# Attention inside a macaron block: TensorE's order of scores, exponents and values in rounds of two units

## The chip, the cores and the metric

The kernel runs on one core of one Trainium2 chip. The metric is the device time of one execution in microseconds (us), median of three runs. A profiled execution gives the trace; its span (first to last instruction) is a little shorter than the device time.

## What is computed

A macaron block on x of shape 8 x 512 x 128: half an attention-and-mixture-of-experts layer, a recurrence, the same half layer again. Cut to the part that the change touches, run twice in the kernel:

```python
def _msa(x, w_qkv, w_proj):              # H = 16 heads of DK = 8, on layer-normed x
    qkv = (x @ w_qkv).reshape(b, n, 3, H, DK)
    q, k, v = ...                        # each b, h, n, d; n = 512
    attn = jnp.einsum('bhnd,bhmd->bhnm', q, k) * (1.0 / np.sqrt(DK))
    attn = jax.nn.softmax(attn, axis=-1)
    y = jnp.einsum('bhnm,bhmd->bhnd', attn, v)
    return y.transpose(0, 2, 1, 3).reshape(b, n, d) @ w_proj
...
x = x + 0.5 * _L0_ffn_ref(_layernorm(x), ...)   # holds _msa and the experts
x = x + _L0_attn_ref(_layernorm(x), ...)        # recurrence, no change here
x = x + 0.5 * _L0_ffn_ref(_layernorm(x), ...)
```

## The kernel before

`attention_phase` (line 461) is written by hand for five engines; each has its own instruction stream, and semaphores join them. Work is cut into batches (8), groups of four heads (4 to a batch, so 32 groups in all, counted by G) and units: unit u of a group is 128 of the 512 keys for the four heads. A step handles one group: its four units' exponents and values, and, two groups ahead, the scores from which the softmax maxima come.

In each unit TensorE (`step`, line 727) issues four pairs and one set of values. Pair n is a score matmul (`score`, line 657: 62 rows, 512 columns, for group G + 2) and an exponent matmul (`exponent`, line 685: 64 rows, 512 columns, for group G). The two use different halves of the array's rows and run beside each other. The values (`pv`, line 691) are four matmuls of 128 rows by 32 columns, one per head, side by side; each stands in the trace as two instructions. In before they come in two halves of 256 columns, `part` 0 and 1. The order in a unit is: pairs 0 and 1, half the values of the unit before, pairs 2 and 3, the other half; in unit 1 the first half comes behind pair 2.

The scores go to four PSUM banks (`psS`, line 500): score h to bank h. VectorE reduces two banks at a time to maxima over 512 (`reduce_pair`, line 830; line 834): first scores 0 and 1, then 2 and 3. Score 0 and score 2 wait for VectorE: lines 659 and 660 let a score into its bank only when the reduction of the same two banks, of the unit before, has ended; `s_read` counts reductions.

The exponents go through a ring of three banks (`RING`, lines 509 to 516), which they share with the turned maxima ("m") and the turned outputs ("o"). ScalarE reads each one and writes probabilities (line 816). The outputs of two groups (`SHARE`) accumulate in bank 7; after them ScalarE copies the bank (`keep_o`, line 787), TensorE turns the copy (`turn_o`, line 709, four transposes), ScalarE copies the result (`copy_o`, line 793), and GpSimd divides by the sums (`normalize`, line 618: a power at line 621 and two products at line 627).

The maxima of a group go through GpSimd (`split_max`, line 608), TensorE (`turn_max`, line 705), ScalarE (`keep_rows`, line 781) and two DMAs of SP (`place`, line 559) into two extra rows of the queries, so that the exponent matmul subtracts them. The exponents of a group wait for that (line 733). In before `turn_max` is at the end of unit 0, `turn_o` at the end of unit 1 of an even group.

Before the first step a prelude computes the scores of groups 0 and 1 alone (lines 715 to 724), with `turn_max(1)` between the two. In the last two groups no scores are left.

Of the kernel before, what the change touches and what calls it, by code (L numbers as in the profile page):

```python
# [13 lines left out]
P = 128  # L14
# [446 lines left out]
def attention_phase(nc, ps, s, v_all, y_all, qd, kd, load=None):  # L461
# [4 lines left out]
    with Phase(nc) as ctx:  # L466
# [13 lines left out]
        neg_wide = sb("neg_wide", [P, P], F32R)  # L480
        neg_parts = neg_wide[:, 0:NMAX].rearrange("p (e a m) -> p e a m", e=2, a=SPLITS)
# [28 lines left out]
        for u in range(TPB):  # L510
            RING += [("e", u, 0), ("e", u, 1)]
            RING += [("e", u, 2), ("e", u, 3)]
            if u == 0:
                RING.append(("m",))
            if u == 1:
                RING.append(("o",))
# [25 lines left out]
        with nc.Block() as block:  # L542
# [46 lines left out]
            def _(pool):  # L589
# [10 lines left out]
                g_.memset(neg_wide[:, NMAX:].bitcast(F32), 0.0).then_inc(v_set, 1)  # L600
# [31 lines left out]
                pool.wait_ge(v_set, NG + 2)  # L632
# [5 lines left out]
                def step(b, g, first, last):  # L638
                    if not first or g > 0:
# [5 lines left out]
                        if g % SHARE == 0:  # L645
                            normalize(bb, gg - 1, shared(b, g))
# [7 lines left out]
            def _(pe):  # L654
# [36 lines left out]
                def pv(g, u, unit, part):  # L691

                    if part == 0:
                        pe.wait_ge(e_read, 4 * unit + 4)
                    here = slice(part * T // 2, (part + 1) * T // 2)


                    for h in range(GROUP):
                        last = t.matmul(psO[VW * h:VW * (h + 1), here], vs[g][:, u, h, :], probs[u % 2][:, h, here],  # L699
                                        start=(g % SHARE == 0 and u == 0 and part == 0),  # L700
                                        stop=(g % SHARE == SHARE - 1 and u == TPB - 1 and part == 1))
                    if part:
                        last.then_inc(pv_unit, 1)

                def turn_max(count):
                    pe.wait_ge(split_done, count)
                    t.transpose(ring("m")[:, 0:P], neg_wide[:].bitcast(F32), s["ident"][:]).then_inc(rows_turned, 1)
# [7 lines left out]
                for i in range(2):  # L715
# [6 lines left out]
                    if i == 0:  # L722
                        pe.wait_ge(v_set, NG + 2)
                        turn_max(1)
                pe.wait_ge(q_set, 3 * NG)

                def step(b, g, first, last):
# [3 lines left out]
                    for u in range(TPB):  # L731
# [10 lines left out]
                        def values(part):  # L742
                            if u > 0:
                                if u == 1 and part == 0:
                                    pe.wait_ge(v_staged, G + 1)
                                    if g % SHARE == 0 and not (first and g == 0):
                                        pe.wait_ge(o_kept, shared(b, g))
                                pv(g, u - 1, unit - 1, part)
                            elif not (first and g == 0):
                                pv((g - 1) % NG, TPB - 1, unit - 1, part)  # L750

                        ahead_score(0)
                        exponent(b, g, first, last, u, 0)
                        ahead_score(1)
                        exponent(b, g, first, last, u, 1)
                        if u != 1:
                            values(0)
                        ahead_score(2)
                        exponent(b, g, first, last, u, 2)
                        if u == 1:  # L760
                            values(0)
                        ahead_score(3)
                        exponent(b, g, first, last, u, 3)
                        values(1)
                        if u == 0 and not (last and g == NG - 1):
                            ring_free(b, g, first, last, "m")
                            turn_max(G + 2)
                        if u == 1 and g % SHARE == 0 and not (first and g == 0):
# [4 lines left out]
                for part in range(2):  # L773
                    pv(NG - 1, TPB - 1, TPB * NG * B - 1, part)
# [1318 lines left out]
```

## Time and profile before

| | |
|---|---|
| device time, median of 3 (range) | 1531.38 us (1530.72 to 1533.6) |
| the profiled execution: span | 1515.8 us |
| TensorE matmul, busy share of the span | 82% |
| VectorE | 70% |
| ScalarE | 56% |
| GpSimd | 43% |
| attention, first to last reduction, first time | 59.9 to 405.2 us |
| attention, first to last reduction, second time | 953.9 to 1299.4 us |

The profiled execution's own time is its span and 15.6 us around it, if it is taken to be the median. Busy time counts an instruction from its recorded start to its recorded end; instructions of an engine can overlap in it, and a group's mean length is then more than the spacing of starts. In rows of a timeline, the first number is the start in us from the start of the span, the second the length of the row's stretch, and "x4" the number of instructions merged in it; "[0.32 <-PE ps L661]" is the engine's idle time before the row and what ended it. PE is TensorE's matmuls, PEld its weight loads, DVE VectorE, ACT ScalarE, POOL GpSimd.

### The profile page before, as it was taken

What the parts mean: (1) busy time and instruction counts of PE and PEld (TensorE: products, weight loads), DVE (VectorE), ACT (ScalarE), POOL (GpSimd) and SP (SyncE); (2) the same over time, 40 slices, a digit from 0 to 9 for tenths busy, and PEclk for the clock granted to TensorE, in tenths of its full rate; (3) what the DMA queues carried; (4) which work ended last, traced back from release to release, by engine and by line L of the source; (5) the groups of instructions that cost most, each with busy time, mean ns of one, the idle gap of its engine ahead of it and who ended that gap; (6) DMA issues with size and microseconds to landing.
All of it is one profiled execution on the core that took longest, in us unless ns stands there. A gap on an engine that the chain in (4) does not pass through costs nothing. (4 is left out here: it accounts for less than half of the span.)

```text
span 1515.8 us, 39418 instructions
## 1 busy us (share of the span) xinstructions
PE 1245.9 (82%) x12592; PEld 708.5 (47%) x12593; DVE 1065.5 (70%) x1896; ACT 851.6 (56%) x1710; POOL 646.5 (43%) x743
## 2 busy tenths in 40 slices
PE   5499999999969497398888746699999999875793
PEld 3234343434349497144454434233443434375793
DVE  8689989998645232468888757799899989264232
ACT  3178888888831253444334214288888888720451
POOL 4312343233336465355765632323432343337362
PEclk9689999999985699599999859599999999965897
DMA  5513342212001121100000005221212111001124
GB/s 177 164 30 78 100 108 60 63 47 55 16 1 34 56 69 45 49 2 3 3 3 2 3 1 224 55 58 46 56 44 57 43 56 44 2 8 61 49 68 122
DMA packets 81640, 81.93 MB, mean 54 GB/s; under 512 B 16265, under 2 KB 53868, under 8 KB 81536
## 3 DMA queue, kind: packets, MB, share of 16 engines
q1 hardware_dynamic: 72704, 70.01, 16.7%
q0 software_dynamic: 4608, 8.44, 1.7%
q10 hardware_dynamic: 4224, 2.10, 0.5%
q8 instruction: 64, 1.05, 0.3%
q14 instruction: 40, 0.33, 0.1%
HBM read 50.56 MB, written 29.93 MB: 53 GB/s over the span
## 5 line engine op out<-in xcount | busy, mean ns | idle before, releaser
L834 DVE TENSOR_REDUCE maxima<-ps 128x2 f32<-128x1024 f32 x512 | 623.9, 1225 | 73.9 <-PE ps L661 68.3
L816 ACT ACTIVATE probs<-ps 128x512 f32<-128x512 f32 x1024 | 552.8, 594 | 92.5 <-PE ps L688 76.2
L661 PE MATMUL ps<-k_stack,q_stack 62*128 62x512 f32 x1024 | 384.4, 474 | 35.2 <-DMA k_stack<-k_split 24.0
L688 PE MATMUL ps<-q_stack,k_stack 64*128 64x512 f32 x1024 | 385.0, 458 | 0.4
L699 PE MATMUL ps<-probs,v_stack 128*32 128x256 f32 x4096 | 329.3, 394 | 1.2 <-ACT probs L816 1.2
L661 PEld LDWEIGHTS ps<-k_stack,q_stack 62*128 62x128 f32 x1024 | 158.6, 194 | 232.8 <-DVE maxima L834 118.2
L621 POOL TENSOR_TENSOR inv<-o_rows,minus_one 128x32 f32<-128x32 f32 x32 | 174.1, 5439 | 132.4 <-ACT o_rows L797 132.4
L688 PEld LDWEIGHTS ps<-q_stack,k_stack 64*128 64x128 f32 x1024 | 160.3, 186 | 15.7 <-ACT probs L816 7.5
L699 PEld LDWEIGHTS ps<-probs,v_stack 128*32 128x32 f32 x4096 | 81.0, 108 | 169.7 <-issue 115.5
L613 POOL CAST neg_wide<-maxima 128x16 fp32r<-128x16 f32 x64 | 12.6, 196 | 302.1 <-DVE maxima L834 302.1
L1314 POOL DMA_INDIRECT expert_out<-yt,number x80 | 78.4, 979 | 69.4 <-POOL number L1310 35.0
L1291 DVE COPY w_now<-w 128x512 f32 x80 | 34.2, 427 | 85.9 <-issue 43.5
L1272 ACT ACTIVATE xT<-ps,ln_b,ln_w 128x128 f32<-128x128 f32 x80 | 36.6, 457 | 95.3 <-PE ps L1243 95.3
L1249 PE MATMUL ps<-xT,w_now 128*128 128x128 f32 x640 | 88.6, 283 | 0.0
L1256 PE MATMUL ps<-w,hidT 128*128 x640 | 85.6, 278 | 0.0
L1249 PEld LDWEIGHTS ps<-xT,w_now 128*128 128x128 f32 x640 | 81.1, 199 | 0.0
L1256 PEld LDWEIGHTS ps<-w,hidT 128*128 128x128 f32 x640 | 79.2, 195 | 0.1
L1172 POOL DMA_INDIRECT sorted<-rows,slot x64 | 62.3, 973 | 18.3 <-issue 15.9
L1277 ACT ACTIVATE hidT<-ps 128x512 f32<-128x512 f32 x80 | 47.8, 598 | 37.0 <-PE ps L1249 37.0
L1746 POOL TENSOR_TENSOR r_kx<-r_kx,r_k_factor 128x512 f32<-128x512 f32 x48 | 61.0, 1271 | 11.4 <-PE ps L1924 7.7
L1727 POOL TENSOR_TENSOR r_mixed<-r_shift,zT 128x512 f32<-128x512 f32 x40 | 59.2, 1487 | 14.2 <-DVE r_shift L1603 14.2
L1243 PE MATMUL ps<-ident,xt 128*128 128x128 f32 x80 | 23.3, 291 | 44.1 <-DMA xt<-sorted 44.1
(204 smaller groups left out, 1673.7 us busy)
## 6 DMA issues: line engine op xcount, KB each, us to landing
q_stack<-q_split SPq DMA_DIRECT2D x256, 64.0 KB
k_stack<-k_split SPq DMA_DIRECT2D x512, 32.0 KB
q_split<-q_parts SPq DMA_DIRECT2D x16, 512.0 KB, 2.7
k_split<-k_parts SPq DMA_DIRECT2D x16, 512.0 KB, 3.4
xt<-sorted SPq DMA_DIRECT2D x80, 64.5 KB
w<-in_L_ffn_w SPq DMA_DIRECT2D x16, 256.0 KB, 3.1
rows<-expert_out SPq DMA_DIRECT2D x16, 256.0 KB, 3.3
x_all<-in_L_attn_x SPq DMA_DIRECT2D x8, 256.0 KB, 3.0
```

What stands on the lines that cost most here:

```text
L621: g_.tensor_tensor(inv[:].rearrange("p q h w -> p (q h w)"), o_rows[:].rearrange("p q h w d -> p (q h w) d")[:, :, DK], minus_one[:].rearr ...
L661: mm = t.matmul(psS[:, h, :], qs[g][score_rows(h), h // 2, u * P:(u + 1) * P], ks[g][score_rows(h), h // 2, :], start=True, stop=True)
L688: t.matmul(ring("e", u, n), ks[g][half(h), h // 2, u * P:(u + 1) * P], qs[g][half(h), h // 2, :], start=True, stop=True).then_inc(e_ready, 1)
L699: last = t.matmul(psO[VW * h:VW * (h + 1), here], vs[g][:, u, h, :], probs[u % 2][:, h, here], start=(g % SHARE == 0 and u == 0 and part = ...
L816: a.activation(probs[u % 2][:, h, :], ring("e", u, n), ACT.Exp, scale=float(DK) ** -0.5).then_inc(e_read, 1)
L834: v.tensor_reduce(maxima[i][:, :, pair, u:u + 1], psS[:, 2 * pair:2 * pair + 2, :], AX_X, ALU.max, negate=True).then_inc(s_read, 1)
L1172: pool.indirect_dma_start(xs, bass.IndirectOffsetOnAxis(ap=slot[:, i:i + 1], axis=0), rows[:, i, :], None).then_inc(scattered, 16)
L1249: last = t.matmul(psH[o][:, c * P:(c + 1) * P], w1_now[o][:, c * P:(c + 1) * P], xT[o][:], start=True, stop=True)
L1256: last = t.matmul(psY[i][:, 0:P], hidT[i][:, c, :], s["w2"][:, ds(second_expert, 1), c, :], start=(c == 0), stop=(c == HC - 1))
L1314: pool.indirect_dma_start(ys, bass.IndirectOffsetOnAxis(ap=number[out_slot][:], axis=0), yt[out_slot][:], None, bounds_check=TOK - 1, oob_ ...
L1727: g.tensor_tensor(mixed[f][:], shift[f % 2][:], x, ALU.add).then_inc(mixed_ready.sem, 1)
L1746: g.tensor_tensor(dst[:].rearrange("p (k m) -> p k m", m=m), src[:].rearrange("p (k m) -> p k m", m=m), k_factor[l][:].rearrange("p n two ...
```

## The change

Five things in `attention_phase`:

- TensorE's order. Two units make a round. Even unit: pairs 0, 1, 2, then all values of the unit before in one block of 512 columns, then pair 3. Odd unit: pairs 0 and 1, half the values, pairs 2 and 3, the other half. In unit 1 of an even group all values come behind pair 3, then the outputs are turned.
- `turn_max` moves from the end of unit 0 to the middle of unit 1, ahead of the values, and turns 32 columns instead of 128 (`neg_wide` shrinks); in the prelude it moves into the scores of group 1. The ring's order follows.
- ScalarE copies the outputs ahead of the last exponential of unit 0, not at the start of unit 1, and the turned maxima ahead of the third exponential of unit 1.
- GpSimd normalizes in the odd group that follows, not in the even group in which the outputs are turned.
- One memset on GpSimd goes, with the count that it stood for.

The diff, cut to its core:

```diff
-        neg_wide = sb("neg_wide", [P, P], F32R)
-        neg_parts = neg_wide[:, 0:NMAX].rearrange("p (e a m) -> p e a m", e=2, a=SPLITS)
+        neg_wide = sb("neg_wide", [P, NMAX], F32R)
+        neg_parts = neg_wide[:].rearrange("p (e a m) -> p e a m", e=2, a=SPLITS)
...
             RING += [("e", u, 0), ("e", u, 1)]
+            if u == 1:
+                RING.append(("m",))
             RING += [("e", u, 2), ("e", u, 3)]
-            if u == 0:
-                RING.append(("m",))
...
-                        if g % SHARE == 0:
-                            normalize(bb, gg - 1, shared(b, g))
+                    if g % SHARE and not (first and g == 1):
+                        bb, gg = (b, g - 2) if g > 1 else (b - 1, NG - 1)
+                        normalize(bb, gg - 1, shared(b, g))
...
-                def pv(g, u, unit, part):
-
-                    if part == 0:
+                def pv(g, u, unit, first, count):
+
+                    if first == 0:
                         pe.wait_ge(e_read, 4 * unit + 4)
-                    here = slice(part * T // 2, (part + 1) * T // 2)
+                    here = slice(first * T // 2, (first + count) * T // 2)
...
-                    t.transpose(ring("m")[:, 0:P], neg_wide[:].bitcast(F32), s["ident"][:]).then_inc(rows_turned, 1)
+                    t.transpose(ring("m")[0:NMAX, 0:P], neg_wide[:].bitcast(F32), s["ident"][:]).then_inc(rows_turned, 1)
...
-                    if i == 0:
-                        pe.wait_ge(v_set, NG + 2)
-                        turn_max(1)
+                        if i == 1 and u == 1:
+                            pe.wait_ge(v_set, NG + 1)
+                            turn_max(1)
...
-                        ahead_score(0)
-                        exponent(b, g, first, last, u, 0)
-                        ahead_score(1)
-                        exponent(b, g, first, last, u, 1)
-                        if u != 1:
-                            values(0)
-                        ahead_score(2)
-                        exponent(b, g, first, last, u, 2)
+                        def pair(n):
+                            ahead_score(n)
+                            exponent(b, g, first, last, u, n)
+
+                        pair(0)
+                        pair(1)
+                        if u % 2 == 0:
+                            pair(2)
+                            if u:
+                                pv(g, u - 1, unit - 1, 0, 2)
                             elif not (first and g == 0):
-                                pv((g - 1) % NG, TPB - 1, unit - 1, part)
...
+                                pv((g - 1) % NG, TPB - 1, unit - 1, 0, 2)
+                            pair(3)
+                            continue
                         if u == 1:
-                            values(0)
-                        ahead_score(3)
-                        exponent(b, g, first, last, u, 3)
-                        values(1)
-                        if u == 0 and not (last and g == NG - 1):
-                            ring_free(b, g, first, last, "m")
-                            turn_max(G + 2)
-                        if u == 1 and g % SHARE == 0 and not (first and g == 0):
+                            pe.wait_ge(v_staged, G + 1)
+                            if not (last and g == NG - 1):
+                                ring_free(b, g, first, last, "m")
+                                turn_max(G + 2)
+                        fresh = u == 1 and g % SHARE == 0
+                        if not fresh:
+                            pv(g, u - 1, unit - 1, 0, 1)
+                        pair(2)
+                        pair(3)
+                        if fresh:
+                            if not (first and g == 0):
+                                pe.wait_ge(o_kept, shared(b, g))
+                            pv(g, u - 1, unit - 1, 0, 2)
+                        else:
+                            pv(g, u - 1, unit - 1, 1, 1)
+                        if fresh and not (first and g == 0):
                             ring_free(b, g, first, last, "o")
                             turn_o(shared(b, g))
...
-                        if u == 1 and g % SHARE == 0 and not (first and g == 0):
-                            keep_o(shared(b, g))
-                        if u == 1 and not (last and g == NG - 1):
-                            keep_rows((g + 1) % 2, G + 2)
...
                         for n, h in enumerate(E_ORDER):
+                            if u == 0 and n == 3 and g % SHARE == 0 and not (first and g == 0):
+                                keep_o(shared(b, g))
+                            if u == 1 and n == 2 and not (last and g == NG - 1):
+                                keep_rows((g + 1) % 2, G + 2)
```

## Rows read from the trace of the kernel before

**Rows 1.** The page's costliest groups: count | busy, mean ns | idle before, releaser.
```profile
L834 DVE TENSOR_REDUCE maxima<-ps 128x2 f32<-128x1024 f32 x512 | 623.9, 1225 | 73.9 <-PE ps L661 68.3
L816 ACT ACTIVATE probs<-ps 128x512 f32<-128x512 f32 x1024 | 552.8, 594 | 92.5 <-PE ps L688 76.2
L661 PE MATMUL ps<-k_stack,q_stack 62*128 62x512 f32 x1024 | 384.4, 474 | 35.2 <-DMA k_stack<-k_split 24.0
...
L699 PE MATMUL ps<-probs,v_stack 128*32 128x256 f32 x4096 | 329.3, 394 | 1.2 <-ACT probs L816 1.2
L621 POOL TENSOR_TENSOR inv<-o_rows,minus_one 128x32 f32<-128x32 f32 x32 | 174.1, 5439 | 132.4 <-ACT o_rows L797 132.4
```
**Rows 2.** Windows: attention, its prelude, and a stretch of the recurrence (last row).
```profile
core 0: us, PE busy (x) PEld busy (x) DVE busy (x) ACT busy (x) POOL busy (x), PEclk, DMA share, GB/s
200.00:250.00 50.00, 49.10 (x459) 20.12 (x461) 45.34 (x38) 42.66 (x84) 17.75 (x24) 1.00 0.38 92
...
61.50:79.00 17.50, 10.78 (x29) 3.85 (x27) 15.38 (x14) 0.27 (x1) 5.54 (x15) 0.50 0.33 63
800.00:840.00 40.00, 32.59 (x780) 18.53 (x779) 35.81 (x65) 14.85 (x47) 26.65 (x20) 1.00 0.01 2
```
**Rows 3.** Timeline of VectorE, prelude and first group.
```profile
67.79 1.21 DVE L834 TENSOR_REDUCE maxima<-ps 128x2 f32<-128x1024 f32 x1
71.12 9.14 DVE L834 TENSOR_REDUCE maxima<-ps 128x2 f32<-128x1024 f32 x8 [2.12 <-PE ps L661]
...
85.52 1.23 DVE L834 TENSOR_REDUCE maxima<-ps 128x2 f32<-128x1024 f32 x1 [1.15 <-PE ps L661]
87.68 1.23 DVE L834 TENSOR_REDUCE maxima<-ps 128x2 f32<-128x1024 f32 x1 [0.94 <-PE ps L661]
```
**Rows 4.** Timeline of TensorE's weight loads, even group, units 0 to 2.
```profile
211.60 0.18 PEld L661 LDWEIGHTS ps<-k_stack,q_stack 62*128 62x128 f32 x1 [0.41 <-issue]
...
212.27 0.16 PEld L699 LDWEIGHTS ps<-probs,v_stack 128*32 128x32 f32 x8 [0.37 <-issue]
212.84 0.14 PEld L707 LDWEIGHTS ps<-ident,neg_wide 128*128 128x128 f32 x1 [0.41 <-ACT probs L816]
213.10 0.18 PEld L661 LDWEIGHTS ps<-k_stack,q_stack 62*128 62x128 f32 x1
...
213.66 0.18 PEld L661 LDWEIGHTS ps<-k_stack,q_stack 62*128 62x128 f32 x1 [0.19 <-DVE maxima L834]
...
214.32 0.16 PEld L699 LDWEIGHTS ps<-probs,v_stack 128*32 128x32 f32 x8 [0.24 <-ACT probs L816]
214.89 0.18 PEld L661 LDWEIGHTS ps<-k_stack,q_stack 62*128 62x128 f32 x1 [0.41 <-issue]
...
215.32 0.16 PEld L699 LDWEIGHTS ps<-probs,v_stack 128*32 128x32 f32 x8 [0.24 <-issue]
215.89 0.42 PEld L712 LDWEIGHTS ps<-ident,oT 128*128 128x128 f32 x4 [0.41 <-issue]
216.47 0.18 PEld L661 LDWEIGHTS ps<-k_stack,q_stack 62*128 62x128 f32 x1 [0.17 <-issue]
```
**Rows 5.** The same view, outputs turned six groups earlier.
```profile
151.12 0.42 PEld L712 LDWEIGHTS ps<-ident,oT 128*128 128x128 f32 x4 [0.41 <-issue]
```
**Rows 6.** Timeline of VectorE, the stretch of rows 4.
```profile
211.23 2.38 DVE L834 TENSOR_REDUCE maxima<-ps 128x2 f32<-128x1024 f32 x2
213.88 1.23 DVE L834 TENSOR_REDUCE maxima<-ps 128x2 f32<-128x1024 f32 x1 [0.27 <-PE ps L661]
215.43 1.23 DVE L834 TENSOR_REDUCE maxima<-ps 128x2 f32<-128x1024 f32 x1 [0.32 <-PE ps L661]
```
**Rows 7.** Timeline of TensorE's matmuls: the last two halves of values, with no work between.
```profile
424.57 1.07 PE L699 MATMUL ps<-probs,v_stack 128*32 128x256 f32 x16 [0.60 <-ACT probs L816]
```
**Rows 8.** Timelines of an odd group: turning of maxima, and VectorE behind it.
```profile
224.28 0.14 PEld L707 LDWEIGHTS ps<-ident,neg_wide 128*128 128x128 f32 x1 [0.77 <-ACT probs L816]
...
225.31 2.49 DVE L834 TENSOR_REDUCE maxima<-ps 128x2 f32<-128x1024 f32 x2 [0.63 <-PE ps L661]
```

More of the change, by code:

```diff
@@ L599, in _ @@
                     g_.memset(vs[i][:], 0.0).then_inc(v_set, 1)
-                g_.memset(neg_wide[:, NMAX:].bitcast(F32), 0.0).then_inc(v_set, 1)
                 g_.memset(minus_one[:], -1.0).then_inc(v_set, 1)
@@ L630, in normalize @@
                     last.then_inc(o_done, 1)
-                pool.wait_ge(v_set, NG + 2)
+                pool.wait_ge(v_set, NG + 1)
                 for g in range(NG):
@@ L689, in exponent @@
                              start=True, stop=True).then_inc(e_ready, 1)
-                def pv(g, u, unit, part):
-                    if part == 0:
+                def pv(g, u, unit, first, count):
+                    if first == 0:
                         pe.wait_ge(e_read, 4 * unit + 4)
-                    here = slice(part * T // 2, (part + 1) * T // 2)
+                    here = slice(first * T // 2, (first + count) * T // 2)
                     for h in range(GROUP):
                         last = t.matmul(psO[VW * h:VW * (h + 1), here], vs[g][:, u, h, :], probs[u % 2][:, h, here],
-                                        start=(g % SHARE == 0 and u == 0 and part == 0),
-                                        stop=(g % SHARE == SHARE - 1 and u == TPB - 1 and part == 1))
-                    if part:
+                                        start=(g % SHARE == 0 and u == 0 and first == 0),
+                                        stop=(g % SHARE == SHARE - 1 and u == TPB - 1))
+                    if first + count == 2:
                         last.then_inc(pv_unit, 1)
@@ L740, in ahead_score @@
                                 score(g2, u, h, 8 * (G + 2) + 2 * u + h // 2)
[L742 to L748, printed above, removed]
-                            elif not (first and g == 0):
-                                pv((g - 1) % NG, TPB - 1, unit - 1, part)
@@ L772, in _ @@
                 bodies(pe, step)
-                for part in range(2):
-                    pv(NG - 1, TPB - 1, TPB * NG * B - 1, part)
+                pv(NG - 1, TPB - 1, TPB * NG * B - 1, 0, 2)
                 turn_o(NG * B // SHARE)
```

## The prediction

> **What bounds the kernel now.** I read the costliest groups first. The reductions to maxima (VectorE), the exponentials (ScalarE) and the matmuls of scores and values, all of the attention phase, head the list [rows 1]. The windows then put numbers on one steady stretch: in 50 us TensorE is busy 49.10, VectorE 45.34, ScalarE 42.66, at the full granted clock [rows 2]. Two engines look like the bound, so the next question is how close VectorE really is. In the prelude, where reductions queue up behind each other, eight of them take 9.14 us and a single one 1.21, so the starts stand (9.14 - 1.21) / 7 = 1.13 apart, although each lasts 1.23 [rows 3]: the last tenth of one lies under the next. VectorE could thus take one every 1.13 us. In the steady stretch they come every 1.24, because TensorE delivers them so: from the first weight load of a run of two pairs to that of the values 0.67 (211.60 to 212.27), from there to the next work 0.57 (212.27 to 212.84), together 1.24 for half a unit [rows 4]. TensorE's order sets the pace now; VectorE has 0.11 to spare on each reduction.
>
> The period of two groups (eight units): the outputs are turned at 151.12 and again at 215.89, six groups later [rows 5, 4]; 64.77 / 3 = 21.59 us. Of that, 16 half units are 19.84; the rest is the turning of maxima (0.26 each, 212.84 to 213.10), that of outputs (0.58, 215.89 to 216.47) and waits.
>
> One of these waits matters most. In the even group's second unit the program before already has a run of three: score 2 is issued there before the first values. At 213.66 its weight load waits for VectorE [rows 4]: the reduction that still reads banks 2 and 3 ends at 211.23 + 2.38 = 213.61 [rows 6]. Score 3 of that unit comes behind the values at 214.89, and the reduction of both starts at 215.43, after an idle 0.32 [rows 4, 6].
>
> **What the change does to TensorE alone.** A run of n pairs costs 0.43 for one (214.89 to 215.32) and 0.67 for two, so 0.24 for each more and 0.91 for three [rows 4]. The values of one unit in a single block are never seen in before. Four sets of four matmuls back to back take 1.07 with 0.38 for the last one's own length [rows 7], a set each 0.23; four sets and the change of shape behind them (0.57 less two sets, 0.11) make 1.03. A wide set saves a start or two, so I take 0.99; bounds are 0.92 (without the 0.11) and 1.14 (two halves of 0.57). A round of two units was 4 x 1.24 = 4.96 and becomes 0.91 + 0.99 + 0.91 + 0.57 + 0.67 + 0.57 = 4.62: one change of shape less, 0.34 saved.
>
> The Trainium skill, "TensorEngine Tiling (Array Packing)", Key Properties, says that changing the tiling mode drains the TensorE. By that rule the round ought to be 0.34 shorter, and the kernel faster (first rival).
>
> **What it does to the hand-over with VectorE.** The scores have four banks: 0 and 1 for scores 0 and 1, 2 and 3 for scores 2 and 3. One reduction reads two banks and needs both scores; score 2 of a unit may not start before the reduction of banks 2 and 3 of the unit before has ended. Before, scores 2 and 3 stand next to each other in three of four units. After, in every even unit (0 and 2), the whole block of values stands between them. So a chain forms that no slack elsewhere shortens, from the end of one reduction of banks 2 and 3 to the start of the next:
> - reduction's end to the weight load of score 2: 213.61 to 213.66, 0.05 [rows 6, 4];
> - that load to the load of the values: a run that starts anew behind a wait costs what a single pair does, 0.43;
> - the block of values: 0.99;
> - the load of score 3 to the reduction: 214.89 to 215.43, 0.54 [rows 4, 6].
> Sum 2.01. During it VectorE has only the reduction of banks 0 and 1, 1.13: it idles some 0.9 in each even unit. The round is then 2.01 plus the three reductions behind it: 1.13 + 1.13 until the next may start, 1.23 for the last, which has to end: 3.49. Round: 5.50, against 4.96 before. With the block at 0.92 it is 5.43; were the spacing 1.23, as busy times suggest, 5.70; with both upper ends 5.85. I take the queued spacing of 1.13, because reductions do queue there.
>
> TensorE needs only 4.62 of the 5.50 and waits for the rest. In the odd unit, score 2 waits until 1.23 + 0.05 = 1.28 after the even unit's second reduction starts; score 3 follows and both are ready well before VectorE has done the next reduction (0.67 - 0.43 + 0.54 = 0.78 later, at 2.06, against 2.26). That part adds nothing.
>
> **The round that turns outputs** (second unit of an even group): counted from the start of the first unit's second reduction, score 2 at 1.28, run of two 0.67, block 0.99, turning of outputs 0.58, run of three 0.91, block 0.99, score 3 to reduction 0.54: 5.96. TensorE is the bound in it.
>
> **The other parts.** Turning the maxima (0.26 or less, 32 columns of weights for 128) moves from a round's open path to a place ahead of score 2, which waits anyway until 1.28: nothing, as long as that wait is there, else 0.26 a group. The copy of turned maxima and that of outputs on ScalarE move by less than a unit; behind them stand exponentials. Eight of these cost at most 8 x 0.594 = 4.75 a round [rows 1], under 5.50: nothing. SP's placing of the maxima waits for that copy and comes about a unit later, ahead of the next loads in SP's queue; its result is wanted at the next group's start: nothing, and if it came late, TensorE would start that group later by as much. The normalization on GpSimd (5.44 for the power [rows 1]) goes to the odd group, where the copies of outputs are long done; behind it on GpSimd stands the splitting of maxima, which waits for the group's last reduction in any case. This removes the odd group's late turning (load at 224.28 behind 0.77 idle, VectorE idle 0.63) [rows 8], a gap that the period of 21.59 contains. The smaller zeroing on GpSimd is at the start, off the path.
>
> The prelude: VectorE's idle 2.12 between the two groups [rows 3] goes, since the turning comes inside the second group's scores: -2.1 per attention. Against it stands the start at the lower clock, where reductions are 2.16 apart (85.52 to 87.68) [rows 3]: a block and a turn of twice the length on the same chain, about +2 (0 to 3) in the first two groups, which also lack one block and one turning of outputs. Both together: nothing.
>
> **Sum.** Two groups: 3 x 5.50 + 5.96 = 22.46, against 21.59: +0.87. Of 32 groups 30 have scores ahead; without the first two that is 14 such periods per attention, 28 in all: 28 x 0.87 = 24.4. The last two groups without scores run at ScalarE's and TensorE's exchange; I leave them. The profiled execution (1515.8 span and 15.6 around it) stands for the median of 1531.38: 1531.4 + 24 = 1555.
>
> **Rivals.**
> 1. Faster: TensorE's own time decides, as now. Then the periods go to two rounds of 4.62, one with a turn of maxima 4.88, and one with both turns and two blocks 0.91 + 0.99 + 0.91 + 0.26 + 0.67 + 0.99 + 0.58 = 5.31: 19.43, or -2.16 x 28 = -60, and -4 in the preludes: 1467. It decides if the four links fit under the 1.13 of one reduction; the block alone takes 0.99. The wait at 213.66 and the idle 0.32 behind a half block speak against it. 0.06. The drain rule above leads here.
> 2. A shorter chain: each round 0.2 less than worked out, by links that overlap, gives 28 x (0.87 - 0.80) = 2 and thus 1533; nothing shows such an overlap. 0.08, half of it below 1528.
> 3. The spacing is 1.23, or the block 1.14: round 5.70 or 5.65, 1572 or 1568. Against the first of the two stands a steady row, two reductions in 2.38 and so 2.38 - 1.23 = 1.15 apart [rows 6]. 0.10.
> 4. TensorE waits more, and its clock falls to 1.2 GHz for part of the phase. It would be busy 4.62 of 5.50, 84%; another stretch at 81% (32.59 of 40) keeps the full clock, while the prelude, with 10.78 of 17.50, is at half [rows 2]. A tenth of the rounds at half would add at least 12 x 4 = 48: 1600. 0.03. The Trainium skill, "TensorE: Matmul & The Clock Gate", section "A second HAM failure mode: psum-queue depth-cycling", describes a kernel whose short idles between groups of matmuls made the clock swing.
>
> **How the numbers follow.** The forecast, 1545 to 1565, has 0.73. The range reaches down to 1540 (block 0.92 and part of the turn hidden) and up to 1575 (third rival). What a measurement can tell from no change is about 0.2%, 3 us. Faster: 0.06 and 0.04, 0.10. Same: 0.04. Slower: the rest, 0.86.
>
> **What would show it.** In the profile after: in every even unit VectorE idles about 0.9 before the reduction of banks 2 and 3 and nothing before the next two; the weight load of score 2 is put down to the reduction; the block of values lasts near 0.99; periods of two groups near 22.5. If periods are below 21.6 with VectorE gap-free, rival 1 holds and my chain is wrong; if the gap is there but the reductions are 1.23 apart, rival 3.

## The result and the profile after

The changed kernel is slower: 1575.1 us, median of four runs (1568.4 to 1580.0), against 1531.05 for the kernel before (four runs, 1529.4 to 1533.6). The ratio is 1.0297, with a 95% interval of 1.0271 to 1.0323. The profiled execution after has a span of 1575.4 and a device time of 1577.2. The forecast was 1555, in a range of 1545 to 1565: the direction is right, but of +44 us it saw +24, and the result lies above the range.

The page's costliest groups first (columns as in [rows 1]):
```profile
L837 DVE TENSOR_REDUCE maxima<-ps 128x2 f32<-128x1024 f32 x512 | 597.2, 1221 | 135.7 <-PE ps L661 135.7
L819 ACT ACTIVATE probs<-ps 128x512 f32<-128x512 f32 x1024 | 543.7, 599 | 122.9 <-PE ps L688 118.1
L661 PE MATMUL ps<-k_stack,q_stack 62*128 62x512 f32 x1024 | 378.5, 468 | 55.3 <-DVE maxima L837 30.8
...
L620 POOL TENSOR_TENSOR inv<-o_rows,minus_one 128x32 f32<-128x32 f32 x32 | 174.1, 5442 | 34.9 <-ACT o_rows L800 34.9
```
All durations are within 2% of [rows 1]; the idle times are not. VectorE idles 135.7 before its reductions where it idled 73.9, all of it put down to the scores, and TensorE's scores wait more for VectorE (30.8 us, in before 11.1). Each of the two waits for the other, more than before. That VectorE's busy time falls from 623.9 to 597.2 at the same length of one reduction (1225 and 1221 ns) is no saving: reductions that queue lie over each other by a tenth (four in 4.69 below start (4.69 - 1.23) / 3 = 1.15 apart and last 1.23), and time in which two lie over each other counts once. GpSimd's wait for the copied outputs is down from 132.4 to 34.9, as the later normalization wants it.

The window of [rows 2] in the steady stretch, columns as there:
```profile
200.00:250.00 50.00, 46.28 (x350) 18.37 (x351) 40.85 (x35) 39.63 (x79) 15.33 (x18) 1.00 0.34 80
```
TensorE falls from 49.10 to 46.28 of 50 and VectorE from 45.34 to 40.85, at the full granted clock: no engine is busy throughout any more.

VectorE's timeline shows the rounds (start, length, then how many reductions queue without a gap, and the idle time ahead of them):
```profile
201.82 4.62 DVE L837 TENSOR_REDUCE maxima<-ps 128x2 f32<-128x1024 f32 x4 [0.53 <-PE ps L661]
207.40 4.69 DVE L837 TENSOR_REDUCE maxima<-ps 128x2 f32<-128x1024 f32 x4 [0.96 <-PE ps L661]
212.91 4.68 DVE L837 TENSOR_REDUCE maxima<-ps 128x2 f32<-128x1024 f32 x4 [0.82 <-PE ps L661]
218.49 3.49 DVE L837 TENSOR_REDUCE maxima<-ps 128x2 f32<-128x1024 f32 x3 [0.90 <-PE ps L661]
223.07 1.23 DVE L837 TENSOR_REDUCE maxima<-ps 128x2 f32<-128x1024 f32 x1 [1.09 <-PE ps L661]
224.83 1.23 DVE L837 TENSOR_REDUCE maxima<-ps 128x2 f32<-128x1024 f32 x1 [0.53 <-PE ps L661]
```
Each row but that at 223.07 begins with the second reduction of an even unit, so the distance of two is a round: 207.40 - 201.82 = 5.58, then 5.51, then 5.58, and the round that turns outputs 224.83 - 218.49 = 6.34. The idle 0.8 to 1.0 stands before the second reduction of an even unit, and nothing before those behind it, as forecast, except behind the turning of outputs (1.09 at 223.07, 0.53 at 201.82 and 224.83). The row at 218.49 has exactly the three reductions of the forecast, and they take the forecast 3.49.

How the 44 us divide, from the starts and ends of these instructions in the two profiled executions (us, each of the two attentions within 0.1):

| stretch of one attention | before | after | difference | forecast |
|---|---|---|---|---|
| first reduction to first exponential (prelude) | 20.25 | 18.04 | -2.2 | -2.1 |
| first exponential to that of the third group | 22.91 | 23.16 | +0.25 | +2 |
| 14 periods of two groups, each | 21.58 | 22.96 | +1.38 | +0.87 |
| last reduction to last exponential (tail) | 19.27 | 21.63 | +2.4 | 0 |
| last exponential to last output | 9.43 | 9.43 | 0 | 0 |

For both attentions the ends of these stretches are 39.4 apart from those before (19.7 each). The other +5 of the medians' +44 lies outside attention, by this account.

### The profile page after: what moved, and what is told of

The parts are those of the page before. It is cut to its first block and busy times, and to the rows that moved or that the text cites. A ratio compares the mean times of both kernels' runs of the same rounds, so it can differ in the third digit from the quotient of the medians.

```text
span 1575.4 us, 36848 instructions
## 1 busy us (share of the span) xinstructions
PE 1254.6 (80%) x11312; PEld 707.7 (45%) x11313; DVE 1042.7 (66%) x1896; ACT 842.1 (53%) x1710; POOL 646.3 (41%) x741
## 5 line engine op out<-in xcount | busy, mean ns | idle before, releaser
L837 DVE TENSOR_REDUCE maxima<-ps 128x2 f32<-128x1024 f32 x512 | 597.2, 1221 | 135.7 <-PE ps L661 135.7
L819 ACT ACTIVATE probs<-ps 128x512 f32<-128x512 f32 x1024 | 543.7, 599 | 122.9 <-PE ps L688 118.1
L661 PE MATMUL ps<-k_stack,q_stack 62*128 62x512 f32 x1024 | 378.5, 468 | 55.3 <-DVE maxima L837 30.8
L688 PE MATMUL ps<-q_stack,k_stack 64*128 64x512 f32 x1024 | 374.1, 459 | 0.3 <-ACT probs L819 0.3
L699 PE MATMUL ps<-probs,v_stack 128*32 128x512 f32 (+1 forms) x2816 | 296.2, 493 | 18.4 <-ACT probs L819 18.4
L661 PEld LDWEIGHTS ps<-k_stack,q_stack 62*128 62x128 f32 x1024 | 168.6, 194 | 297.6 <-DVE maxima L837 155.5
L620 POOL TENSOR_TENSOR inv<-o_rows,minus_one 128x32 f32<-128x32 f32 x32 | 174.1, 5442 | 34.9 <-ACT o_rows L800 34.9
L688 PEld LDWEIGHTS ps<-q_stack,k_stack 64*128 64x128 f32 x1024 | 168.0, 187 | 25.7 <-ACT probs L819 14.0
L699 PEld LDWEIGHTS ps<-probs,v_stack 128*32 128x32 f32 x2816 | 55.5, 108 | 122.8 <-ACT probs L819 66.8
L1299 DVE COPY yt<-ps 128x128 f32<-128x128 f32 x80 | 23.3, 292 | 51.8 <-PE ps L1259 51.1
```

The source lines that it names most:

```text
L620: g_.tensor_tensor(inv[:].rearrange("p q h w -> p (q h w)"), o_rows[:].rearrange("p q h w d -> p (q h w) d")[:, :, DK], minus_one[:].rearr ...
L661: mm = t.matmul(psS[:, h, :], qs[g][score_rows(h), h // 2, u * P:(u + 1) * P], ks[g][score_rows(h), h // 2, :], start=True, stop=True)
L688: t.matmul(ring("e", u, n), ks[g][half(h), h // 2, u * P:(u + 1) * P], qs[g][half(h), h // 2, :], start=True, stop=True).then_inc(e_ready, 1)
L819: a.activation(probs[u % 2][:, h, :], ring("e", u, n), ACT.Exp, scale=float(DK) ** -0.5).then_inc(e_read, 1)
L837: v.tensor_reduce(maxima[i][:, :, pair, u:u + 1], psS[:, 2 * pair:2 * pair + 2, :], AX_X, ALU.max, negate=True).then_inc(s_read, 1)
```

## The experiments

All kernels are edits of the kernel before or after; ratios are to runs of the kernel before on the same chip. "Period" is two groups, "round" is two units, both averaged over an attention (median or mean moves them by a few hundredths). e4 and e6 to e9 are single executions: their device times have no interval, and they are read by periods.

**e1: break the chain at score 3.** In even units of after, score 3 goes ahead of the block of values; its exponent stays behind.
```diff
                             pair(2)
+                            ahead_score(3)
                             if u:
                                 pv(g, u - 1, unit - 1, 0, 2)
...
-                            pair(3)
+                            exponent(b, g, first, last, u, 3)
...
```


> The changed kernel with one move: in even units score 3 is issued ahead of the block of values, its exponent stays behind it. As many changes of shape, as many matmuls, ScalarE and GpSimd untouched. Theory (the block between scores 2 and 3 makes VectorE wait): the idle 0.96 us before the second reduction of even units goes, the chain is about 0.9 instead of 2.09, TensorE sets the pace again at 4.62 + 0.24 (score 3 without a partner) a round; two groups take about 20.8 instead of 22.96, device time about 1515 us. Rival (wider block, ScalarE's moved copies or the turn in mid-round make it slow): the period stays within 0.3 of 22.96 or rises by the lone score, 4 x 0.24 = 1 us, device time 1575 to 1600.

Measured: 1582.4, ratio 1.0355 (1.0326 to 1.0385), period 23.31. The expectation failed, though the idle 0.96 on VectorE fell to 0.2. Three rounds are at 5.21, 5.77 and 5.47, together 0.2 less than in after; the turning round is at 6.82 for 6.30. The weight loads, with the matching rows of VectorE and ScalarE behind them, show why:
```profile
202.73 0.19 PEld L688 LDWEIGHTS ps<-q_stack,k_stack 64*128 64x128 f32 x2 [0.84 <-ACT probs L820]
...
203.92 0.16 PEld L699 LDWEIGHTS ps<-probs,v_stack 128*32 128x32 f32 x8 [0.66 <-ACT probs L820]
204.49 0.18 PEld L661 LDWEIGHTS ps<-k_stack,q_stack 62*128 62x128 f32 x1 [0.41 <-issue]
...
206.55 0.18 PEld L661 LDWEIGHTS ps<-k_stack,q_stack 62*128 62x128 f32 x1 [0.52 <-DVE maxima L838]
...
208.28 0.19 PEld L688 LDWEIGHTS ps<-q_stack,k_stack 64*128 64x128 f32 x2 [0.84 <-ACT probs L820]
...
205.27 3.59 DVE L838 TENSOR_REDUCE maxima<-ps 128x2 f32<-128x1024 f32 x3 [0.49 <-PE ps L661]
...
203.27 1.58 ACT L820 ACTIVATE probs<-ps 128x512 f32<-128x512 f32 x3 [0.65 <-PE ps L688]
```
Exponent 3 is loaded behind the block (202.73), ScalarE begins on it at 203.27, and the next values may not start before it is through (203.92). Only behind those come the odd unit's scores 2 and 3 (204.49), their reduction (205.27), the next score 2 (206.55), and a block again (from 207.28 to 208.28): 208.28 - 202.73 = 5.55. There is a second loop, through ScalarE and VectorE, nearly as long as the first. What I had put in the list of parts as "nothing" (exponentials "under 5.50") is no chain by its sum of 4.75, but it is one by the place of exponent 3.

**e2: halves in even units again.** Pairs 0 to 2, half the values, pair 3, the other half.
```diff
                             if u:
-                                pv(g, u - 1, unit - 1, 0, 2)
+                                pv(g, u - 1, unit - 1, 0, 1)
...
                             pair(3)
+                            if u:
+                                pv(g, u - 1, unit - 1, 1, 1)
...
```


> The changed kernel with the block of even units cut in two: half behind pair 2, half behind pair 3, so four changes of shape a round as in the kernel before. Theory: the chain loses half a block, 0.43, so each round that the chain sets becomes 0.43 shorter (5.58 to 5.15), the round that turns outputs less; two groups about 21.6 us, device time about 1540. Rival (what counts is TensorE's changes of shape): one more change in each round, 4 x 0.34 longer, two groups 24.3, device time about 1612.

Measured: 1571.5, ratio 1.0283 (1.0246 to 1.0319), period 23.09: neither number. The chain from one reduction's end to the next one's start did become shorter, 1.66 in place of 2.09, but the rounds only 5.36 (odd group, into the second even unit 5.50), and the turning round grew from 6.30 to 6.84, which eats what the others gain. Between an odd unit's score 3 and the next even unit's score 2 stand a half and two pairs of TensorE's work, 1.48; the reduction needs 0.44 (until it starts) + 1.23 + 0.05 = 1.72 there. As the third pair of its run, score 2 comes too early whatever stands behind it, and TensorE waits in order.

**e5: score 3 and exponent 3 both ahead of the block**, the edit that shortens both loops.
```diff
                             pair(2)
+                            pair(3)
                             if u:
                                 pv(g, u - 1, unit - 1, 0, 2)
...
-                            pair(3)
```


> The changed kernel with all of pair 3 (score and exponent) ahead of the block of values in even units; still three changes of shape a round. Enlarged theory: TensorE issues in order, and two waits go round with the block: score 2, third in a run, waits for a reduction that started only 0.44 after the last score 3, and the next values wait for ScalarE to read exponent 3, which stands behind the block. This edit takes away the second and the block between scores 2 and 3, and leaves a wait of score 2 of about 0.3 a round: round 4.63 + 0.3 to 0.4, about 5.0; two groups 21.4 to 21.8 us, device time 1525 to 1540. Rival (the wide block itself, or fewer changes of shape, cost more than their rows say): two groups stay at 22.9 or more.

Measured: 1562.6, ratio 1.0229 (1.0190 to 1.0269), period 22.55 where 21.4 to 21.8 was expected. Three rounds are at 5.10, 5.12 and 5.38, near the 5.0 expected: with both loops cut the 5.5 goes. The round that turns outputs missed: 6.96. There `keep_o` stands in ScalarE's queue ahead of exponential 3, which is now ready before the block ends, and the copy needs the block:
```profile
215.53 0.60 ACT L794 ACTIVATE oT<-ps 128x512 f32<-128x512 f32 x1 [0.70 <-PE ps L699]
```

**e6 and e7: reductions over half the columns**, in after and in before. The maxima are those of the first 256 of 512 keys; the rest of the kernel is whole.
```diff
-  psS[:, 2 * pair:2 * pair + 2, :], AX_X,
+  psS[:, 2 * pair:2 * pair + 2, 0:T // 2], AX_X,
```


> The changed kernel with reductions over 256 of the 512 columns: the maxima are those of half the keys, all else is as it was. A reduction then lasts about 0.69 instead of 1.23. Theory (score 2 waits for VectorE): that wait goes, what is left is the values' wait for ScalarE; rounds of 5.58 become about 4.9, the round that turns outputs stays at 6.3; two groups 21.1 instead of 22.96. Rival (VectorE is not in the loop): two groups within 0.2 of 22.96.

> The kernel before with the same half reductions (maxima of half the keys). Theory: TensorE alone sets the pace there, so the period of two groups stays within 0.3 of 21.58, lower only by the waits of score 2 in the second unit of even groups. Rival (VectorE, busy 0.9, is a second bound): the period falls by 1 us or more.

Measured: in before the period stays at 21.58 (1516.4 us, a shorter prelude and less elsewhere): VectorE was no bound there, as read from [rows 4, 6]. In after the period falls from 22.96 to 21.49 and the rounds into a unit 0 from 5.58 to 4.91, the odd group's other one from 5.50 to 5.35 (1524.8 us); the turning round stays at 6.32. (21.1 was expected; the odd group's other round makes the difference.) So the lost time runs through the reductions, except in the turning round. The group of reductions in e6, and one load of values:
```profile
L837 DVE TENSOR_REDUCE maxima<-ps 128x2 f32<-128x512 f32 x512 | 342.0, 690 | 337.7 <-PE ps L661 337.7
...
200.18 0.16 PEld L699 LDWEIGHTS ps<-probs,v_stack 128*32 128x32 f32 x8 [0.68 <-ACT probs L819]
```
VectorE is out of the way, and the rounds are still 4.91, not TensorE's 4.62: the values wait for ScalarE.

**e8: the outputs' copy twice on ScalarE** (after, with a spare tile).
```diff
+                    a.activation(oT_more[:], psO, ACT.Copy)
                     a.activation(oT[:], psO, ACT.Copy).then_inc(o_kept, 1)
```


> The changed kernel with ScalarE's copy of the outputs made twice (the first into a spare tile). It stands ahead of exponential 3 of the first unit of even groups. Theory (this copy delays exponentials 3, 0 and 1, by these the bank for exponent 3 and so the second block): the round that turns outputs grows by the 0.48 of one more copy, 6.30 to 6.78, the others stay at 5.50 to 5.58. Rival (ScalarE has slack, as the prediction had it): nothing changes.

Measured: the turning round goes from 6.30 to 6.79, the others stay at 5.50 to 5.58, the period is 23.45 (1593.3 us). ScalarE in one such round:
```profile
196.86 0.60 ACT L795 ACTIVATE oT_more<-ps 128x512 f32<-128x512 f32 x1 [0.40 <-PE ps L700]
197.35 0.59 ACT L796 ACTIVATE oT<-ps 128x512 f32<-128x512 f32 x1
197.83 1.58 ACT L821 ACTIVATE probs<-ps 128x512 f32<-128x512 f32 x3
```
The second copy begins 0.49 after the first and puts the exponentials back by 0.48; the round grows by 0.49, the whole of it. ScalarE's copy lies on the path of this round.

**e3 and e11: the change without its order** (the same kernel twice, e11 in more runs): before, with the normalization a group later and the turn of maxima inside the prelude's second group, and nothing else.
```diff
-                        if g % SHARE == 0:
-                            normalize(bb, gg - 1, shared(b, g))
+                    if g % SHARE and not (first and g == 1):
+                        bb, gg = (b, g - 2) if g > 1 else (b - 1, NG - 1)
+                        normalize(bb, gg - 1, shared(b, g))
...
-                    if i == 0:
...
+                        if i == 1 and u == 1:
...
+                            turn_max(1)
```


> The kernel before with two parts of the change alone: normalization on GpSimd in the odd group, and the turning of maxima in the prelude inside the second group's scores. TensorE's order in the steps is that of before. Theory: the late turning of maxima in odd groups goes, VectorE's idle 0.62 there falls to about 0.26 (the turn itself), two groups 21.59 to about 21.2; the first exponential of each attention comes 2.2 us earlier; device time 1531 - 30 x 0.18 - 4.4, about 1521. Rival (GpSimd's lateness was hidden by other waits): period unchanged, 1527 from the prelude alone.

> Kernel e3 again, in more rounds and on the same chip as e10: about 1516 us, 0.9901 of the kernel before, interval inside 0.985 to 0.995; two groups 21.31 us.

Measured: 1516.5, ratio 0.9901 (0.9866 to 0.9936), and 1514.9, ratio 0.9914 (0.9895 to 0.9934): faster than both kernels, and about 1% under the kernel before. The period is 21.31 in both, the prelude 18.04 as in after. 28 x (21.58 - 21.31) = 7.6 and 2 x 2.2 make 12 of the 13 to 15 us. GpSimd in an odd group of e3, and VectorE behind the turning of maxima, in this group (223.79) and in the even one that follows (234.03):
```profile
223.32 5.45 POOL L621 TENSOR_TENSOR inv<-o_rows,minus_one 128x32 f32<-128x32 f32 x1
...
231.48 0.20 POOL L613 CAST neg_wide<-maxima 128x16 fp32r<-128x16 f32 x1 [1.60 <-DVE maxima L835]
...
223.79 9.97 DVE L835 TENSOR_REDUCE maxima<-ps 128x2 f32<-128x1024 f32 x8 [0.27 <-PE ps L662]
234.03 1.23 DVE L835 TENSOR_REDUCE maxima<-ps 128x2 f32<-128x1024 f32 x1 [0.27 <-PE ps L662]
```
The power is over well before the group's last reduction, the splitting waits for VectorE alone (1.60 idle), and VectorE's 0.63 of [rows 8] is down to 0.27. Both parts are in after too, so what its order costs has to be measured against e3: 22.96 - 21.31 = 1.65 a period, or 46 us in 28.

**e10: e3, with the odd group's unit 1 in the even order of halves** (`values(0)` behind pair 1 there too).

> Kernel e3 (before with the normalization in odd groups and the turn inside the prelude) with one more edit: in unit 1 of odd groups the first half of the values goes behind pair 1, as in units 0, 2 and 3, so that no run of three is left there. Theory (a run of three makes score 2 wait): VectorE's idle 0.09 before the second reduction of that unit goes; two groups 21.31 to about 21.2 us, 3 us in the device time. Rival (what counts is the number of changes of shape, equal in both): no difference.

Measured: 1526.1, ratio 0.9977 (0.9960 to 0.9994), period 21.45, slower than e3's 21.31 on the same chip. The idle 0.09 that it aimed at goes to 0.01, but 0.235 appears before the second reduction of unit 2: the gap moves on and grows. The 28 x 0.14 = 4 us of the periods and 1 us in the two tails are less than half of the 11 us between e10 and e11; the rest was not traced.

**e9: halves in the last two groups of after**, which have no scores.
```diff
+                        if not ahead:
+                            prior = (g, u - 1) if u else ((g - 1) % NG, TPB - 1)
+                            pair(0)
+                            pair(1)
...
+                            else:
+                                pv(*prior, unit - 1, 0, 1)
+                            pair(2)
...
+                            pair(3)
+                            pv(*prior, unit - 1, 1, 1)
...
```
(In unit 1 the first half comes behind pair 2, and the turns and the copies stand where after has them.)

> The changed kernel, but in the last two groups, which have no scores ahead, the values go in halves as in the kernel before (behind pair 1, or behind pair 2 in unit 1, and behind pair 3). Theory (the block and the later turn leave ScalarE idle in this tail): the time from the last reduction to the last exponential falls from 21.6 to about 19.3 us, all else stays. Rival (a spell at the lower clock after the last reduction is to blame, whatever the order): it stays above 21.

Measured: the tail falls from 21.63 to 20.37, about half of the way back to 19.27 (1567.9 us). But the granted clock moved with it. The tails of after, e9 and e1 (columns of [rows 2]; the clock is the third number from the end):
```profile
422.87:444.50 21.63, 19.19 (x122) 6.45 (x121) 0.00 (x0) 17.34 (x35) 6.65 (x5) 0.92 0.01 2
```
```profile
422.29:442.64 20.35, 18.18 (x159) 7.11 (x155) 0.00 (x1) 17.83 (x35) 6.65 (x5) 1.00 0.01 2
```
```profile
427.40:447.92 20.52, 17.89 (x123) 6.04 (x122) 0.00 (x0) 17.52 (x35) 6.66 (x5) 1.00 0.01 2
```
e1 changes nothing where no scores are left, so in these groups it has after's order, block and all; at the full clock its tail is 20.52. Of after's 2.4, the lower clock is thus about 1.1 (the rival, for half of the loss), and the halves of e9 give back only some 0.15. The two attentions of e8, of the same code, say the same of the clock: 23.60 with 6.8 us at 0.50, 20.82 with none.

**e4: the kernel before once more**, for what lies outside attention.

> The kernel before once more, for the stages outside attention. From the profiles of before and after they differ by 20 us (middle 519.9 to 534.5, end 187.7 to 193.2) though the change does not touch them. If that is the granted clock of the recurrence in one execution, this run's middle part lies between 520 and 535 with as many spells at the lower clock; if it came from the change, it repeats 519.9 within 1 us.

Measured: span 1529.5, device time 1531.4, period 21.58. The stretch between the attentions is 526.3, against 519.9 in the first profile of the same kernel, and the end 193.8 against 187.7. So of the 20 us by which the first profiles of before and after differ there, 12.5 stand between two executions of one kernel.

## Why the prediction missed its range, and what of it was right

**The bound before: right.** e7 halves VectorE's work and the period stays at 21.58: TensorE's order, not VectorE's busy 45 of 50, set the pace.

**The chain: right, one link 0.08 short.** The weight loads of after, the odd group's unit 2 and then group boundary to the turning of outputs:
```profile
210.94 0.18 PEld L661 LDWEIGHTS ps<-k_stack,q_stack 62*128 62x128 f32 x1 [0.21 <-DVE maxima L837]
210.94 0.18 PEld L688 LDWEIGHTS ps<-q_stack,k_stack 64*128 64x128 f32 x1
211.38 0.16 PEld L699 LDWEIGHTS ps<-probs,v_stack 128*32 128x32 f32 x8 [0.25 <-ACT probs L819]
...
216.45 0.18 PEld L661 LDWEIGHTS ps<-k_stack,q_stack 62*128 62x128 f32 x1 [0.65 <-DVE maxima L837]
216.53 0.18 PEld L688 LDWEIGHTS ps<-q_stack,k_stack 64*128 64x128 f32 x1
216.96 0.16 PEld L699 LDWEIGHTS ps<-probs,v_stack 128*32 128x32 f32 x8 [0.24 <-ACT probs L819]
217.95 0.18 PEld L661 LDWEIGHTS ps<-k_stack,q_stack 62*128 62x128 f32 x1 [0.84 <-issue]
...
219.77 0.18 PEld L661 LDWEIGHTS ps<-k_stack,q_stack 62*128 62x128 f32 x1 [0.37 <-DVE maxima L837]
...
220.29 0.18 PEld L688 LDWEIGHTS ps<-q_stack,k_stack 64*128 64x128 f32 x1
220.72 0.16 PEld L699 LDWEIGHTS ps<-probs,v_stack 128*32 128x32 f32 x8 [0.25 <-issue]
221.72 0.42 PEld L712 LDWEIGHTS ps<-ident,oT 128*128 128x128 f32 x4 [0.84 <-issue]
222.30 0.18 PEld L661 LDWEIGHTS ps<-k_stack,q_stack 62*128 62x128 f32 x1 [0.17 <-issue]
...
222.87 0.18 PEld L688 LDWEIGHTS ps<-q_stack,k_stack 64*128 64x128 f32 x1
223.30 0.16 PEld L699 LDWEIGHTS ps<-probs,v_stack 128*32 128x32 f32 x8 [0.24 <-issue]
```
Score 2 waits for VectorE and is loaded at 216.45; values at 216.96; score 3 behind the block at 217.95, 0.99 later; the reduction at 218.49, 0.54 later. The estimate of 0.99 for a block, which no row of before held, and the 0.54 stand. The run costs 0.51, not the 0.43 of a single pair: here the exponent's load comes 0.08 after its score's (216.53), while in the odd group's unit 2 the two come together (210.94) and the run costs 0.44. So rounds into a unit 0 are 5.58 and the odd group's other one 5.50, twice 0.08 a period. Rival 3 falls: three queued reductions take 3.49, and the block 0.99.

The chain by itself was not the whole cause. I called it one that no slack elsewhere shortens, which holds; but in e1 I took its removal to be the cure, and e1 shows a second loop of 5.55 through exponent 3 and ScalarE behind it. Of the edits to the order only e5, which cuts both, brings rounds down to 5.1.

**The round that turns outputs: the mis-sized term.** Forecast 5.96, measured 6.30 (6.34 in the one shown). The step that failed is "the copy of turned maxima and that of outputs on ScalarE move by less than a unit; [...] nothing", which weighed ScalarE's sum against the round. What counts is where the copies stand. ScalarE in that round:
```profile
218.17 0.60 ACT L794 ACTIVATE oT<-ps 128x512 f32<-128x512 f32 x1 [0.46 <-PE ps L699]
218.66 1.57 ACT L819 ACTIVATE probs<-ps 128x512 f32<-128x512 f32 x3
220.09 0.26 ACT L788 ACTIVATE max_rows<-ps 32x128 fp32r<-32x128 f32 x1
...
222.41 0.41 ACT L800 ACTIVATE o_rows<-ps 128x288 f32<-128x288 f32 x1 [0.94 <-PE ps L712]
```
`keep_o` can start only once the block has ended (218.17) and goes ahead of three exponentials, 3 of unit 0 and then 0 and 1 of unit 1, which end at 220.23. The last exponent of unit 1 needs the bank that they read and is loaded at 220.29, so the run of two in front of the block takes 220.72 - 219.77 = 0.95, not 0.67: +0.28. Behind the turning, the third pair of the next run waits for a bank until `copy_o` has ended (222.41 + 0.41 = 222.82, load at 222.87): 1.00, not 0.91: +0.09. The block (1.00) and the turning (0.58) are as forecast. e8 confirms it: 0.49 more copy, 0.49 more round. In e6 this round alone stays at 6.3, so VectorE has no part in it.

**The period** misses by 1.38 - 0.87 = 0.51: 0.34 of the turning round and 2 x 0.08 of the others. Times 28: 14 of the 20 us that the forecast lacked.

**The normalization and the prelude: right.** e3 keeps these two and the old order, and is 0.9% faster; the prelude lost 2.2 where 2.1 was said.

**The first two groups: overestimated**, +0.25 in place of +2 at the lower clock. How long the lower clock lasts there differs from one execution to the next: the same stretch of the kernel before is 21.9 and 24.1 in the two attentions of e4. At equal time at the lower clock (7.1 us) after has 23.16 and e3 22.39, so some +0.8. With the preludes the profiles have 4 us less than forecast, which hides a part of the other misses.

**The tail: left at 0 without a reason, and +2.4 in each attention.** One stretch of it after, first the window 427 to 430 (columns of [rows 2]), then a load and ScalarE's copy in it, and last the same copy in before and in e1:
```profile
427.00:430.00 3.00, 3.00 (x15) 1.19 (x7) 0.00 (x0) 0.57 (x2) 0.16 (x1) 0.50 0.02 5
```
```profile
428.19 0.72 PEld L712 LDWEIGHTS ps<-ident,oT 128*128 128x128 f32 x4 [1.58 <-issue]
...
429.35 0.41 ACT L800 ACTIVATE o_rows<-ps 128x288 f32<-128x288 f32 x1 [2.19 <-PE ps L712]
```
```profile
410.45 0.41 ACT L797 ACTIVATE o_rows<-ps 128x288 f32<-128x288 f32 x1 [0.56 <-PE ps L712]
```
```profile
432.88 0.41 ACT L801 ACTIVATE o_rows<-ps 128x288 f32<-128x288 f32 x1 [0.98 <-PE ps L712]
```
A block and the turning of outputs stand back to back in TensorE's queue, and ScalarE, busy 17.68 of 19.28 in this tail in before, has nothing to read for 2.19 where it had 0.56. The granted clock is 0.50 there (the 1.2 GHz level), and the four loads take 0.72 for 0.42; in e1, with the same order at the full clock, the wait is 0.98. I wrote that the last groups "run at ScalarE's and TensorE's exchange; I leave them". That left out two things: about 1.1 for the lower clock that both attentions of this profile have for 3.4 us, and about 1.25 for the change at the full clock (20.52 - 19.27). e9 takes some 0.15 of the latter away with the block; the moved copies and the moved turn of maxima, which e9 and e1 share, are what is left, and were not tried one by one. Why the clock falls in some of these tails and not in others, no run here shows.

**TensorE's own time decides (rival 1): not so, and its saving was real.** A block takes 0.99 and two halves 1.14 (2 x 0.57). That fits the drain rule of the Trainium skill, "TensorEngine Tiling (Array Packing)", Key Properties, but a block also has half as many matmuls, and no run here parts the two. Even with VectorE out of the way (e6) the period is 21.49, against 21.58 before and 21.31 in e3, which has the later normalization too: two rounds are at 4.91 where before has 4.97 and 4.94, the odd group's other one at 5.35 for 5.56, and the turning round at 6.32 for 6.10. In the rounds of 4.91 and in the turning round waits for ScalarE eat what is saved. Rival 2 needed shorter links, and the links are longer. Rival 4 did not come in the steady stretch, where the clock is 1.00; it came for 3.4 us in each tail of this profile.

**The base.** I took the profiled execution as 1515.8 and 15.6 around it. After has 1577.2 - 1575.4 = 1.8 around its span, and e4 1531.4 - 1529.5 = 1.9: the rest was a difference between executions, mostly outside attention. It did not move the forecast, which added a difference to the median.

**Open: some +5 outside attention.** The recurrence, whose code is the same, lasts 268.4 and 268.9 us in two profiles of before, with 64 and 71 us of it at the lower clock, and 273.5 after, with 79. Among the kernels that keep after's order it is 273 to 275 in four (e1, e5, e6, e8; 75 to 84 us at the lower clock) and 270 to 271 in two (e2, e9; 65 to 70); with before's order it is 266 to 269 (e3, e7, e10, e11). Among kernels of one order the time goes up with the time at the lower clock, but not only with it: at 65 to 71 us of it after's order has 270 to 271 and before's 268 to 269. Neither this nor why the clock should follow the order of an earlier stage is shown by any run here.

## What to carry to other kernels

A saving on the engine that sets the pace counts only if every hand-over in its order still fits: for each wide block, list what stands right behind it, who waits for that, and what comes back to the block, and close the loop through each other engine in turn, not only through the nearest. When one engine's sum of work is under the period, its instructions still cost as much as they delay the next one in its queue; a copy moved ahead of work that others wait for is a term of the sum. Parts of a change that take a wait off the path (the later normalization here) are worth having by themselves: e3 is the kernel to keep.

## What was not expected of the hardware

- Two engines can each be idle for a part of a stretch and the kernel still be bound by their exchange: TensorE is at 46.28 and VectorE at 40.85 of 50 in after, with rounds of 5.58, and behind the first loop stands a second of 5.55, so that cutting one alone (e1) gave 0.2 in three rounds and lost 0.5 in the fourth.
- A weight load that starts behind a wait is followed by its partner's load 0.08 later in unit 0 (216.45, 216.53), at once in the odd group's unit 2; what makes the difference was not tried.
- The same kernel's stretch between the attentions differs by 6 us between two profiles (519.9 and 526.3), nearly as much as the later normalization saves over all 28 periods (7.6); only a look at the stages told the two apart.
- The same code's tail is 23.60 with 6.8 us at the lower clock and 20.82 with none, in the two attentions of one execution (e8): a difference between two profiles of a short stretch says little of the code until the granted clock of both is read.
